# Sum columns ordered by kind, so that a product between two graph layers skips its zero blocks

## The chip, the cores and the metric

One NeuronCore of one Trainium2 chip runs the whole program. The metric is the time of one execution on the device in microseconds. The kernel before takes 9425.36 us (median of three runs, 9407.82 to 9427.2). Engines are named as in the profile: PE is TensorE (PEld its weight loads), DVE is VectorE, ACT is ScalarE, POOL is GpSimd, SP is SyncE.

## What is computed

Two message-passing layers over a graph of 12500 nodes with 160 features (64 scalars and 32 vectors of 3) and 212500 edges. Cut to what matters, the first layer is:

```python
h = max(layernorm(x), 0)                       # per node
f0, f1 = h_scalars @ Wl1_0, h_vectors @ Wl1_1  # per node
w = silu(edge_scalars @ Wfc1) @ Wfc2           # per edge, 192 numbers: w0, w1, w2, w3
mid0 = w0 * f0[src] * sh0                      # 64 scalars          -> n0
mid1 = w3 * sum_m(f1[src] * sh1) / sqrt(3)     # 32 scalars          -> n1
mid2 = w1 * f0[src] x sh1                      # 64 vectors of 3     -> n2
mid3 = w2 * f1[src] * sh0                      # 32 vectors of 3     -> n3
n0..n3 = sums over the edges of a node / max(count, 1)
scal, vec = [n0, n1], [n2, n3]
alpha = scal @ Wa                              # 1 number
conv = [scal @ Wl2_s, vec @ Wl2_v per m]       # 64 and 3 x 32 numbers
x = x + skip(h) + alpha * conv
```

So the scalar outputs (and alpha) come from the scalar sums alone, and component m of the vector outputs from component m of the vector sums alone. The second layer has the same form with other products.

## The kernel before

The program runs in stages. First the edges are sorted by node for the first layer (`sort_edges`): GpSimd scatters edge rows, with their filter weights already computed, to DRAM with indirect DMAs. Then `messages` of the first layer goes over 928 tiles of 256 edges: VectorE makes a one-hot matrix of the edges' nodes and products of weights and gathered features in the tile `prod`, ScalarE makes the outer products (L1689), and TensorE sums them by node (L1637), 449 columns at once: these are the sum columns. VectorE adds the results up in `acc`, and ScalarE's queue stores them as rows of `agg_tab`. Beside that GpSimd gathers features (L1554) and already scatters three quarters of the second layer's edge rows (L1571).

The stage between the layers, `middle`, handles 98 blocks of 128 nodes and, with them, the last 52 chunks (1024 edges each) of the second layer's sort. One step is one block; a chunk is spread over two steps, an even and an odd one. In each step a block's sums (449 columns, padded with zeros to 512) are transposed in four pieces of 128 columns (L1169), moved to SBUF by ScalarE (L1223), and multiplied with `w_out0` (L1178): four f32 products that accumulate 161 output columns, each against 128 rows of weights. Most of these weights are zeros, because each sum column feeds only some outputs. VectorE makes the scale alpha from output column 160 (L1377), adds the outputs to x (L1384, L1385), and takes the layer norm of the new x (L1348, L1359, L1371); TensorE turns the result (L1187, L1188) and makes the node features (L1195, L1196).

The order on each engine is fixed by the code: TensorE's step is transposes of block b, for an even step the rank counts (L416) and the hidden product of the next chunk (L1130), product of block b-1 (L1178), two weight products of the chunk's halves (L488), node turn of block b-3, node product of block b-4. VectorE's step begins with `prepare`: in an even step the bin products, their sum, the next bin one-hot and its count (L350, L360, L330, L341), about 5 us; in an odd step small operations. Then come count, statistics, alpha and `add_conv` of block b-1. There is one PSUM bank for the outputs, so a product waits for `x_done`, VectorE's last use of the one before; alpha waits for `mm_ready`, the product. ScalarE evicts the weight products (L1229), and GpSimd then scatters the chunk with 8 indirect DMAs (L1119).

Which sum column stands where is set by names: in the kernel before, columns 0 to 95 are mid3, 96 to 159 mid0, 160 the count (`ones_at`), 161 to 352 mid2 (`outer_at`), 353 to 448 mid1 (`inner_at`). The weight rows are placed accordingly by `weight_loads`; its helper `rows_into` splits a block of weights that crosses a multiple of 128 rows into two DMAs. SyncE issues these DMAs (L597) at the start, ahead of the sort's first edge data. The last product of the second layer, in `node_sums` (L2011), already runs on column ranges (`L1.spans`), ten passes a block.

Of the kernel before, what the change touches and what calls it, by code (L numbers as in the profile page):

```python
# [21 lines left out]
ALU = mybir.AluOpType  # L22
# [57 lines left out]
S0, V0 = 64, 96  # L80
D = S0 + V0
# [9 lines left out]
L0 = Layer()  # L91
# [4 lines left out]
L0.skip_cols = (64, 96)  # L96
L0.agg = 449
L0.pw = 452
L0.ones_at, L0.outer_at, L0.inner_at = 160, 161, 353
L0.out_cols = 161  # L100
L0.kchunks = [128] * 4
L0.hot_bufs, L0.prod_bufs, L0.res_bufs, L0.add_lag = 4, 4, 3, 4
L0.accs, L0.stores, L0.store_lag = 6, 2, 6

# [134 lines left out]
def weight_loads(t, g):  # L239

    placed = []

    def rows_into(l, row, src, col):

        n, done = src.shape[0], 0
        while done < n:
            r = row + done
            k = min(n - done, P - r % P)
            placed.append((g.w_out[l.n][r % P:r % P + k, r // P, col:col + src.shape[1]], src[done:done + k, :]))
            done += k  # L250

    rows_into(L0, 96, t["L0_gnn_Wl2_s"][0:64, :], 0)
    rows_into(L0, 96, t["L0_gnn_Wa"][0:64, :], 160)
    for m in range(3):
        rows_into(L0, 32 * m, t["L0_gnn_Wl2_v"][64:96, :], 64 + 32 * m)
        rows_into(L0, L0.outer_at + 64 * m, t["L0_gnn_Wl2_v"][0:64, :], 64 + 32 * m)
        rows_into(L0, L0.inner_at + 32 * m, t["L0_gnn_Wl2_s"][64:96, :], 0)
        rows_into(L0, L0.inner_at + 32 * m, t["L0_gnn_Wa"][64:96, :], 160)
    sums_row = lambda group, q: 320 * L1.bank_of[group] + 64 * q + 32 * L1.turn_of[group]
    for q in range(2):  # L260
        rows_into(L1, sums_row(0, q), t["L1_gnn_W_out_s"][32 * q:32 * q + 32, :], 0)
    for k in range(3):
        rows_into(L1, sums_row(0, 2 + k), t["L1_gnn_W_out_v"][64:96, :], 96 + 32 * k)
        for q, (what, j) in enumerate(L1.hots[k][0::2]):
            row = sums_row(k + 1, q)
            if what == "p":
                rows_into(L1, row, t["L1_gnn_W_out_v"][32 * j:32 * j + 32, :], 96 + 32 * k)
            elif what == "3":
                rows_into(L1, row, t["L1_gnn_W_out_s"][64:96, :], 0)
            else:  # L270
                i = 3 - j - k
                plus = (i, j, k) in ((0, 1, 2), (1, 2, 0), (2, 0, 1))
                rows_into(L1, row, t["L1_gnn_W_out_v"][96:128, :] if plus else g.neg_cross[:, :], 96 + 32 * i)
    for l, (feat, skip) in ((L0, ("L0_gnn_Wl1_1", "L0_gnn_Wsc1")), (L1, ("L1_gnn_W_nl1", "L1_gnn_W_skip1"))):
        for m in range(3):
            placed.append((g.wn_v[l.n][m:V0:3, 32 * m:32 * m + 32], t[feat]))
            placed.append((g.wn_v[l.n][m:V0:3, V0 + 32 * m:V0 + 32 * m + 32], t[skip]))
    fc = []
    for l, name1, name2 in ((L0, "L0_gnn_Wfc1", "L0_gnn_Wfc2"), (L1, "L1_gnn_W_fc1", "L1_gnn_W_fc2")):
        for h in range(2):  # L280
            fc.append((g.w1[l.n][h * l.fc_in:(h + 1) * l.fc_in, 64 * h:64 * h + 64], t[name1]))
            col = 0
            for a, b in l.w_cols:
                fc.append((g.w2[l.n][64 * h:64 * h + 64, col:col + b - a], t[name2][:, a:b]))
                col += b - a
    plain = [(g.wn_s[0][:, 0:S0], t["L0_gnn_Wl1_0"]), (g.wn_s[0][:, S0:], t["L0_gnn_Wsc0"]),
             (g.wn_s[1][:, L1.skip_cols[0]:], t["L1_gnn_W_nl0"]), (g.wn_s[1][:, 0:L1.skip_cols[0]], t["L1_gnn_W_skip0"])]
    return fc, plain, placed
# [702 lines left out]
def middle(nc, t, g):  # L991
# [3 lines left out]
    nk = len(L0.kchunks)  # L995
# [15 lines left out]
    with ExitStack() as ctx:  # L1011
# [7 lines left out]
        aggT = [sb(f"aggT{s}", [P, nk, P], F32) for s in range(2)]  # L1019
# [30 lines left out]
        agg_bank, res = g.ps2[1][:, 0, :], g.ps2[1][:, 1, :]  # L1050
# [76 lines left out]
        def _(pe):  # L1127
# [44 lines left out]
            def product(step, it, s):  # L1172
                b = it * DEEP + s
                pe.wait_ge(aT_ready, b + 1)
                if step is None or step >= 1:
                    pe.wait_ge(x_done, b)
                for k, n in enumerate(L0.kchunks):
                    mm = pe.matmul(res[:, 0:L0.out_cols], aggT[s % 2][0:n, k, :], g.w_out[0][0:n, k, :],  # L1178
                                   start=(k == 0), stop=(k == nk - 1))
                mm.then_inc(mm_ready, 1)  # L1180

            def node_turn(step, it, s):
# [106 lines left out]
        def _(dve):  # L1289
# [89 lines left out]
            def add_conv(step, it, s):  # L1379
                b, c, _ = held(step, it, s)  # L1380
                dve.wait_ge(chain, 4 * b + 4)
                xs = g.x_sb[:, bass.ds(b, 1), 0:S0].rearrange("p o d -> p (o d)")
                xv = g.x_sb[:, bass.ds(b, 1), S0:D].rearrange("p o (v m) -> p (o m) v", m=3)
                dve.scalar_tensor_tensor(xs, res[:, 0:S0], c[:, 3:4], xs, ALU.mult, ALU.add)  # L1384
                dve.scalar_tensor_tensor(xv, res[:, S0:D].rearrange("p (m v) -> p m v", m=3), c[:, 3:4], xv,  # L1385
                                         ALU.mult, ALU.add).then_inc(x_done, 1)

            def inverse_root(step, it, s):
# [21 lines left out]
def messages(nc, t, l, g):  # L1410
# [3 lines left out]
    with ExitStack() as ctx:  # L1414
# [3 lines left out]
        def sem(name):  # L1418
# [13 lines left out]
        hot_ready, hot_scaled, prod_ready, sum_ready, acc_ready, iota_made = (  # L1432
            sem(x) for x in ("hot_ready", "hot_scaled", "prod_ready", "sum_ready", "acc_ready", "iota_made"))
        if sends:
# [24 lines left out]
            res = [b[:, 0:l.agg].rearrange("p (o c) -> p o c", o=1)  # L1459
                   for b in (g.ps[0], g.ps[1], g.ps2[1][:, 0, :])]  # L1460
# [319 lines left out]
        def _(dve):  # L1780
# [112 lines left out]
            def other_products(step, it, s):  # L1893
                u = it * TURN + s
                out_p = prod[s % prods]
                _, _, scalars, vectors = forms(s)
                if sends:
                    half = part[s % 2]
                    vectors(0, 0, 0, 3, 1)
                    scalars(32, 96, 1).then_inc(prod_ready, 1)  # L1900
                    dve.wait_ge(part_ready, u * 2 + 2)
                    dve.tensor_tensor(  # L1902
                        out_p[:, :, l.inner_at:l.inner_at + V0].rearrange("p k (m c) -> p k m c", m=3),
                        half[:, :, S0:].rearrange("p k (m c) -> p k m c", m=3),
                        rows[s % HELD][:, :, l.sh_at:l.sh_at + 3].bitcast(F32).rearrange("p k (m o) -> p k m o", o=1)
                        .to_broadcast([P, ST_TILES, 3, 32]), ALU.mult).then_inc(inner_ready, 1)
                else:
                    p0 = l.pieces_at
                    vectors(192, p0, 0, 3, 3)
                    vectors(160, p0 + 160, 0, 2, 3)  # L1910
                    vectors(160, p0 + 32, 2, 3, 1).then_inc(prod_ready, 1)
# [262 lines left out]
```

## Time and profile before

| | |
|---|---|
| Time, median of three runs | 9425.36 us (9407.82 to 9427.2) |
| Span of the profiled execution | 9425.4 us |
| Time of the profiled execution | 9425.36 us |
| Mean granted TensorE clock | 0.831 |
| Sort of the first layer | to about 2200 us |
| First layer's messages | about 2230 to 6150 us |
| Between the layers | about 6180 to 6780 us |
| Second layer's messages | about 6830 to 9230 us |
| Second layer's node sums | to the end |

The profile is one execution. Busy times of engines overlap, so they don't add up to the span. A row of a group gives busy time and mean duration, then the idle time of its engine just before these instructions and what ended it ("<-issue" where no wait explains it). A matmul's duration includes the time to run through the array, so that several in a row start closer together than they last. The granted clock is the share of TensorE's full speed: 1.0 is 2.4 GHz and 0.5 is 1.2 GHz.

### The profile page before, as it was taken

To read this page: it belongs to the slowest core of one execution; us is meant where nothing else is said; L and a number is where in the kernel's file an instruction comes from. 1 tells how busy PE (TensorE), PEld (TensorE's weight loads), DVE (VectorE), ACT (ScalarE), POOL (GpSimd) and SP (SyncE) were. 2 spreads that over 40 slices of the span, in tenths; PEclk is the share of its full clock that TensorE was granted. 3 is DMA by queue.
4 is the path that set the end of the run, shared out by engine and by line. 5 is a ranking of instruction groups with operands and counts; after the bars stand their busy time and mean duration, and the time that the engine had idled before them with its cause. 6 is when DMAs were issued, how large, how long until landed. Compare 5 with 4: busy or idle time off the path is not lost. (4 is left out here: it accounts for less than half of the span.)

```text
span 9425.4 us, 173139 instructions
## 1 busy us (share of the span) xinstructions
PE 6599.8 (70%) x31166; PEld 4418.9 (47%) x31166; DVE 7175.1 (76%) x21240; ACT 4951.0 (53%) x16490; POOL 6782.0 (72%) x6877
## 2 busy tenths in 40 slices
PE   5566565654655565555555556678799999999999
PEld 3333333332222222222222222356588888888888
DVE  7666666665777676767777778977699999999995
ACT  3444444443444444444444445644477777777774
POOL 5777777777777777777777776456677777777770
PEclk7565555657888888888888888989899999999999
DMA  3222222225666666666666666545556666666667
GB/s 105 93 91 93 92 92 92 92 90 165 212 215 212 212 211 213 212 212 212 212 213 214 212 213 205 182 146 171 155 165 167 167 169 168 167 168 169 170 167 229
DMA packets 1189742, 1589.17 MB, mean 169 GB/s; under 512 B 452520, under 2 KB 967336, under 8 KB 1189544
## 3 DMA queue, kind: packets, MB, share of 16 engines
q1 hardware_dynamic: 789976, 836.56, 29.0%
q0 software_dynamic: 328704, 651.74, 24.2%
q10 hardware_dynamic: 70992, 100.14, 3.0%
q8 instruction: 20, 0.33, 0.0%
q14 instruction: 50, 0.41, 0.0%
HBM read 999.62 MB, written 1050.39 MB: 217 GB/s over the span
## 5 line engine op out<-in xcount | busy, mean ns | idle before, releaser
L1656 PE MATMUL pair<-prod_m,hot_m 128*128 128x160 f32 x14848 | 2245.1, 304 | 164.3 <-DVE prod_m L1862 128.1
L1543 POOL DMA_INDIRECT feat_m<-feat_tab,rows_m x1856 | 1830.9, 986 | 579.0 <-issue 441.9
L1656 PEld LDWEIGHTS pair<-prod_m,hot_m 128*128 128x128 f32 x14848 | 2043.6, 190 | 365.9 <-issue 361.3
L1677 ACT ACTIVATE hot_m<-hot_m,rows_m 128x128 f32<-128x128 f32 x5568 | 1728.5, 389 | 700.7 <-DVE hot_m L1845 694.8
L1554 POOL DMA_INDIRECT fetched_m<-feat_tab,index_m x1664 | 1673.2, 1006 | 518.5 <-issue 501.2
L663 POOL DMA_INDIRECT sorted_rows<-rows_e,place_e x1664 | 1611.6, 969 | 539.5 <-issue 503.9
L1689 ACT ACTIVATE prod_m<-part_m,rows_m 128x64 f32<-128x64 f32 x5568 | 1432.3, 337 | 1018.6 <-DVE part_m L1882 864.9
L1571 POOL DMA_INDIRECT sorted_rows<-later_m,place_m x1248 | 1243.9, 997 | 523.8 <-issue 376.4
L1637 PE MATMUL bank<-prod_m,hot_m 128*128 128x449 f32 x2476 | 1111.8, 572 | 575.6 <-DVE prod_m L1902 320.9
L1862 DVE TENSOR_TENSOR prod_m<-rows_m,feat_m 128x192 f32<-128x192 f32 (+2 forms) x4640 | 1282.7, 308 | 0.0
L488 PE MATMUL pair<-fc,hT_m 64*128 64x224 f32 x2496 | 405.5, 454 | 963.8 <-ACT later_m L1732 952.2
L1637 PEld LDWEIGHTS bank<-prod_m,hot_m 128*128 128x128 f32 x2476 | 435.7, 195 | 1304.0 <-issue 1075.4
L1923 DVE SCALAR_TENSOR_TENSOR acc_m<-acc_m,same_block,pair 128x640 f32<-128x640 f32 (+1 forms) x1237 | 1016.8, 822 | 2.3 <-PE pair L1656 2.2
L1732 ACT ACTIVATE later_m<-pair 128x448 f32<-128x448 f32 x624 | 301.8, 535 | 1077.6 <-DMA sorted_rows<-later_m,place_m 1074.7
L488 PEld LDWEIGHTS pair<-fc,hT_m 64*128 64x128 f32 x2496 | 262.5, 228 | 1185.4 <-ACT later_m L1732 1035.9
L1855 DVE TENSOR_TENSOR prod_m<-rows_m,feat_m 128x128 f32<-128x128 f32 x2784 | 709.1, 281 | 101.0 <-DMA feat_m<-feat_tab,rows_m 99.2
L1831 DVE CAST later_m<-meta_m 128x8 f32<-128x8 int32 x156 | 31.3, 200 | 946.8 <-DMA sorted_rows<-later_m,place_m 946.8
L1637 PE MATMUL pair<-prod_m,hot_m 128*128 128x449 f32 x1236 | 720.3, 717 | 39.2 <-DVE prod_m L1902 37.7
L488 PE MATMUL pair<-fc,hT_e 64*128 64x192 f32 x3328 | 602.2, 539 | 0.8 <-ACT rows_e L692 0.8
L416 PE MATMUL bank<-bin_count_e,upper_bf 128*128 128x100 bf16 x207 | 53.5, 259 | 780.5 <-DVE bin_prod_e L350 780.5
L488 PEld LDWEIGHTS pair<-fc,hT_e 64*128 64x128 f32 x3328 | 499.5, 324 | 198.2 <-issue 197.5
L1119 POOL DMA_INDIRECT sorted_rows<-later_c,place_c x416 | 415.3, 998 | 219.5 <-issue 123.0
(264 smaller groups left out, 10303.2 us busy)
## 6 DMA issues: line engine op xcount, KB each, us to landing
agg_tab<-acc_m ACTq DMA_DIRECT2D x928, 320.0 KB
rows_m<-sorted_rows SPq DMA_DIRECT2D x928, 229.0 KB
agg_tab<-acc_m ACTq DMA_DIRECT2D x928, 224.5 KB
rows_m<-sorted_rows SPq DMA_DIRECT2D x928, 197.0 KB
feat_m<-feat_sorted SPq DMA_DIRECT2D x928, 160.0 KB
feat_sorted<-fetched_m SPq DMA_DIRECT2D x208, 640.0 KB, 5.3
turned_m<-in_turned ACTq DMA_DIRECT2D x159, 256.0 KB
agg_s<-agg_tab SPq DMA_DIRECT2D x98, 320.0 KB
```

Source lines behind the costliest of these rows:

```text
L488: return pe.matmul(out, hT[h, k % HALF * P:(k % HALF + 1) * P], g.w2[l.n][h, :], start=True, stop=True)
L663: pool.indirect_dma_start(out=g.sorted_rows[0], out_offset=bass.IndirectOffsetOnAxis(ap=place[s][:, k:k + 1], axis=0), in_=rows[s][:, k, : ...
L1543: pool.indirect_dma_start(out=feat[s % RING][:, k, :], out_offset=None, in_=g.feat_tab[l.n], in_offset=bass.IndirectOffsetOnAxis(ap=rows[s ...
L1554: pool.indirect_dma_start(out=fetched[q][:, k, :], out_offset=None, in_=g.feat_tab[0], in_offset=bass.IndirectOffsetOnAxis(ap=index[q][:, ...
L1571: pool.indirect_dma_start(out=g.sorted_rows[1], out_offset=bass.IndirectOffsetOnAxis(ap=place[h][:, k:k + 1], axis=0), in_=later[h][:, k, ...
L1637: mm = pe.matmul(out[:, 0, :], hot[s % l.hot_bufs][:, k, 0, :], prod[s % prods][:, k, 0:l.agg], start=(k == 0), stop=(k == ST_TILES - 1))
L1656: mm = pe.matmul(dst, hot[s % l.hot_bufs][:, k, q, :], rhs, start=(k == 0 and q < 2), stop=(k == ST_TILES - 1), skip_group_check=True)
L1677: ins = act.activation(hot[s % l.hot_bufs][:, k, 1 + q, :], hot[s % l.hot_bufs][:, k, 0, :], ACT.Copy, scale=rows[s % HELD][:, k, l.sh_at ...
L1689: ins = act.activation(prod[s % prods][:, k, at:at + S0], part[s % 2][:, k, 0:S0], ACT.Copy, scale=rows[s % HELD][:, k, l.sh_at + m:l.sh_a ...
L1855: return dve.tensor_tensor(out_p[:, :, pcol:pcol + 64 * d].rearrange("p k (q c) -> p k q c", q=2)[:, :, :, 0:32], w[:, :, wcol:wcol + 64]. ...
L1862: return dve.tensor_tensor(out_p[:, :, pcol:pcol + 32 * d * n].rearrange("p k (m c) -> p k m c", m=n)[:, :, :, 0:32], w[:, :, wcol:wcol + ...
L1923: dve.scalar_tensor_tensor(half(acc[q]), half(prev), same, res[s % l.res_bufs], ALU.mult, ALU.add).then_inc(acc_ready, 1)
```

## The change

The sum columns are put in another order: mid2 (outer) in 0 to 191, mid3 in 192 to 287 (`vec_at`), mid1 (inner) in 288 to 383, mid0 in 384 to 447 (`scal_at`) and the count in 448. The outputs are reordered too: the 96 vector outputs come first, then the 64 scalar outputs, then alpha's column 160. Each piece of 128 sum columns now reaches only a range of outputs, and the product is limited to it: 64, 96, 97 and 65 columns, 322 in all, where it was four times 161. The first product starts the accumulation with only the first 64 output columns. VectorE's operations and the weight placement follow the new order.

```diff
-L0.ones_at, L0.outer_at, L0.inner_at = 160, 161, 353
+L0.ones_at, L0.outer_at, L0.vec_at, L0.inner_at, L0.scal_at = 448, 0, 192, 288, 384
 L0.out_cols = 161
 L0.kchunks = [128] * 4
+L0.spans = [(0, 64), (0, 96), (64, 161), (96, 161)]
...
-    rows_into(L0, 96, t["L0_gnn_Wl2_s"][0:64, :], 0)
-    rows_into(L0, 96, t["L0_gnn_Wa"][0:64, :], 160)
+    rows_into(L0, L0.scal_at, t["L0_gnn_Wl2_s"][0:64, :], V0)
+    rows_into(L0, L0.scal_at, t["L0_gnn_Wa"][0:64, :], D)
     for m in range(3):
-        rows_into(L0, 32 * m, t["L0_gnn_Wl2_v"][64:96, :], 64 + 32 * m)
-        rows_into(L0, L0.outer_at + 64 * m, t["L0_gnn_Wl2_v"][0:64, :], 64 + 32 * m)
-        rows_into(L0, L0.inner_at + 32 * m, t["L0_gnn_Wl2_s"][64:96, :], 0)
+        rows_into(L0, L0.vec_at + 32 * m, t["L0_gnn_Wl2_v"][64:96, :], 32 * m)
+        rows_into(L0, L0.outer_at + 64 * m, t["L0_gnn_Wl2_v"][0:64, :], 32 * m)
+        rows_into(L0, L0.inner_at + 32 * m, t["L0_gnn_Wl2_s"][64:96, :], V0)
         rows_into(L0, L0.inner_at + 32 * m, t["L0_gnn_Wa"][64:96, :], 160)
...
-                    mm = pe.matmul(res[:, 0:L0.out_cols], aggT[s % 2][0:n, k, :], g.w_out[0][0:n, k, :],
-                                   start=(k == 0), stop=(k == nk - 1))
+                    a, z = L0.spans[k]
+                    mm = pe.matmul(res[:, a:z], aggT[s % 2][0:n, k, :], g.w_out[0][0:n, k, a:z],
+                                   start=(k == 0), stop=(k == nk - 1), skip_group_check=True)
...
-                dve.scalar_tensor_tensor(xs, res[:, 0:S0], c[:, 3:4], xs, ALU.mult, ALU.add)
-                dve.scalar_tensor_tensor(xv, res[:, S0:D].rearrange("p (m v) -> p m v", m=3), c[:, 3:4], xv,
+                dve.scalar_tensor_tensor(xs, res[:, V0:D], c[:, 3:4], xs, ALU.mult, ALU.add)
+                dve.scalar_tensor_tensor(xv, res[:, 0:V0].rearrange("p (m v) -> p m v", m=3), c[:, 3:4], xv,
...
-                    vectors(0, 0, 0, 3, 1)
-                    scalars(32, 96, 1).then_inc(prod_ready, 1)
+                    vectors(0, l.vec_at, 0, 3, 1)
+                    scalars(32, l.scal_at, 1).then_inc(prod_ready, 1)
```

## Rows read from the trace of the kernel before

**Rows 1.** Page, part 1: busy time, share of the span, instructions per engine.

```profile
PE 6599.8 (70%) x31166; PEld 4418.9 (47%) x31166; DVE 7175.1 (76%) x21240; ACT 4951.0 (53%) x16490; POOL 6782.0 (72%) x6877
```

**Rows 2.** Busy time by stage: PE, PEld, DVE, ACT, POOL, then clock, DMA, GB/s.

```profile
2230.00:6150.00 3920.00, 2349.53 (x6812) 1036.15 (x6812) 2896.01 (x8441) 1822.69 (x6658) 2894.02 (x2889) 0.85 0.68 210
...
6180.00:6780.00 600.00, 498.11 (x2776) 361.08 (x2775) 459.15 (x1616) 282.01 (x745) 394.31 (x396) 0.91 0.55 166
```

**Rows 3.** The costliest groups of the whole span: GpSimd's scatters.

```profile
L663 POOL DMA_INDIRECT sorted_rows<-rows_e,place_e x1664 | 1611.6, 969 | 539.5 <-issue 503.9
...
L1119 POOL DMA_INDIRECT sorted_rows<-later_c,place_c x416 | 415.3, 998 | 219.5 <-issue 123.0
```

**Rows 4.** Who waited for whom, 6170 to 6800 us: total, times, longest.

```profile
POOL sorted_rows L1119 <- ACT later_c L1229: 91.4, 35, 15.0
...
DVE bin_prod_c L350 <- PE bank L416: 70.5, 51, 3.9
...
PE pair L1178 <- DVE x_sb L1385: 53.1, 36, 3.0
...
DVE cnt_c L1377 <- PE pair L1178: 32.8, 47, 2.5
```

**Rows 5.** Timeline of an odd step at full clock: start, duration, instruction, idle before.

```profile
6434.78 1.34 PE L1178 MATMUL pair<-w_out,aggT_c 128*128 128x161 f32 x8 [0.83 <-DVE x_sb L1385]
...
6436.05 1.03 PE L488 MATMUL pair<-fc,hT_c 64*128 64x224 f32 x8
...
6436.16 0.28 DVE L1377 TENSOR_SCALAR cnt_c<-pair,cnt_c 128x1 f32<-128x1 f32 x1 [0.24 <-PE pair L1178]
...
6439.19 0.99 DVE L350 TENSOR_TENSOR bin_prod_c<-bin_hot_c,bank 128x800 f32<-128x800 bf16 x1 [0.46 <-PE bank L416]
```

**Rows 6.** Timeline of an odd step at half clock.

```profile
6408.80 2.48 PE L1178 MATMUL pair<-w_out,aggT_c 128*128 128x161 f32 x8 [2.12 <-DVE x_sb L1385]
```

**Rows 7.** Busy time of three whole cycles, product to product, columns as before.

```profile
6408.80:6423.59 14.79, 13.48 (x56) 9.62 (x57) 9.63 (x37) 5.76 (x16) 9.61 (x10) 0.67 0.50 154
...
6423.59:6434.78 11.19, 9.13 (x56) 6.63 (x57) 8.76 (x34) 5.70 (x17) 6.49 (x6) 1.00 0.57 161
...
6434.78:6446.15 11.37, 9.11 (x57) 6.63 (x57) 9.70 (x37) 5.67 (x16) 8.56 (x9) 1.00 0.63 190
```

**Rows 8.** Groups of instructions: both products, with counts, durations, first and last starts.

```profile
L1178 PE MATMUL pair<-w_out,aggT_c 128*128 128x161 f32 x784 | 146.1, 335 | 53.1 <-DVE x_sb L1385 53.1
...
L1178 PE MATMUL pair<-w_out,aggT_c x784: 297/301/608, 6183.2 to 6766.8; 128*128 128x161 f32 x196
...
L2011 PE MATMUL bank<-w_out,aggT_s 128*128 128x160 f32 x392 | 88.6, 308 | 0.0
...
L2011 PE MATMUL bank<-w_out,aggT_s 128*128 128x96 f32 x588 | 78.9, 270 | 0.0
```

**Rows 9.** Timeline: an even step's product, and the second layer's last, one block each.

```profile
6402.68 1.26 PE L1178 MATMUL pair<-w_out,aggT_c 128*128 128x161 f32 x8
...
9300.26 1.38 PE L2011 MATMUL bank<-w_out,aggT_s 128*128 128x160 f32 x10
```

**Rows 10.** Timeline of the start: weight DMAs, first wait for data, first scatter.

```profile
33.93 0.80 SPq L597 DMA_DIRECT2D w_out<-in_L_gnn_Wl_s  x2
...
41.78 0.42 SPq L597 DMA_DIRECT2D w_out<-in_L_gnn_Wa  x1
...
63.81 0.17 DVE L800 COPY first_sh_e<-meta_e 128x8 f32<-128x8 f32 x1 [2.29 <-DMA meta_e<-in_meta]
...
84.07 1.14 POOL L663 DMA_INDIRECT sorted_rows<-rows_e,place_e  x1 [30.30 <-DVE rows_e L803]
```

**Rows 11.** Groups in the first layer's messages: writes to even and odd columns.

```profile
L1902 DVE TENSOR_TENSOR prod_m<-part_m,rows_m 128x192 f32<-128x192 f32 x928 | 325.1, 350 | 0.0
...
L1883 DVE TENSOR_TENSOR part_m<-rows_m,feat_m 128x192 f32<-128x192 f32 x928 | 324.7, 350 | 0.0
...
L1689 ACT ACTIVATE prod_m<-part_m,rows_m 128x64 f32<-128x64 f32 x5568 | 1432.3, 337 | 1018.6 <-DVE part_m L1882 864.9
```

## The prediction

> **What bounds the kernel now.** I read the totals of the page first [rows 1]. VectorE, TensorE and GpSimd are each busy for 70 to 76% of the span, which says only that different stages have different limits, so next came the busy time by stage [rows 2]. The change touches two stages with its steady work: the first layer's messages (2230 to 6150 us) and the stage between the layers (about 6180 to 6780 us).
>
> In the sort before them and in the first layer's messages GpSimd is the limit. One indirect DMA of the sort takes 969 ns and the idle time before the 1664 of them is nearly all "issue", 503.9 us or 0.30 us each [rows 3]: 1664 x 1.27 = 2116 us, the whole stage. In the messages GpSimd has 2889 operations for 2894 us [rows 2]; with the same 0.30 us behind each that is 3761 of 3920 us. TensorE and VectorE have a quarter or more of their time free there.
>
> Between the layers no engine is full: in 600 us TensorE is busy 498, VectorE 459, GpSimd 394, and the granted clock is 0.91 [rows 2]. So it is a loop of waits, and the view to read is who waited for whom [rows 4]. GpSimd waits 35 times for ScalarE's eviction, 91.4 us. VectorE waits 51 times, 70.5 us, for the count products (L416), and 47 times, 32.8 us, for the product between the layers (L1178); TensorE in turn waits 36 times, 53.1 us, for VectorE's update of x (L1385) before that product. A cycle covers two blocks and one chunk. The timeline of one odd step shows the circle [rows 5]: the product starts at 6434.78 and is followed at once on TensorE by the weight products (6436.05), the node turns, the transposes and the counts, and VectorE's bin product (6439.19) waits for those counts. From there VectorE has some 7 us of its own work until it has updated x for the odd block, and only then can the next even block's product start. The first product starts at 6183.2 and the last at 6766.8 [rows 8]: 583.6 / 97 x 2 = 12.03 us per cycle, 49 cycles.
>
> Thus the product of an odd step (even blocks) lies on the loop with its full length: it is ahead of the counts on TensorE's queue. The product of an even step (odd blocks) runs beside VectorE's long work and is free, except where the clock is low.
>
> **Part 1: the product.** It is 8 passes (4 chunks of sums, and each f32 product is two passes: 784 for 98 blocks [rows 8]). At full clock the 8 take 1.26 us [rows 9] where a single one is 301 ns [rows 8]; right behind a wait they take 1.34 [rows 5]. The pace is (1.26 - 0.30) / 7 = 0.137 us a pass of 161 columns. Now the passes get 64, 96, 97 and 65 columns. How short can a pass be that must also load 128 columns of weights? The second layer's last product has the answer: 10 passes, four of 160 and six of 96 columns, take 1.38 us [rows 9], one lasts 0.27 to 0.31. That leaves 1.08 us for 9 intervals; three of them belong to 160 columns at 0.137, so the other six are (1.08 - 0.41) / 6 = 0.11 us. Scaling by columns would have given 0.08. So there is a floor from the weight loads, and passes of 64 columns lie on it too.
>
> Saved per product: 7 x (0.137 - 0.11) = 0.19 us, and 0.03 to 0.08 us at the end of the last pass, which is shorter (160 against 96 columns: 308 against 270 ns is the nearest comparison [rows 8]). I take 0.25 us. The bounds: zero, if the passes keep their pace, and 7 x 0.067 + 0.08 = 0.55 us, if a pass costs only its columns (0.137 / 161 = 0.00085 us each, 80 on average, half of today's pace). The value near the weight floor is nearest to an actual row of the same kind of product. The Trainium skill says the same of this floor: in "TensorE: Matmul & The Clock Gate", section "LDWEIGHTS (loading the stationary operand)", a load lasts its columns divided by 1.2, about 107 ns for 128; this trace agrees with its 0.11. The same page's step on filling the array says that throughput is N cycles; by that alone the saving would be the upper bound, and the row of 96 columns speaks against it.
>
> At half clock everything doubles (2.48 us for the product [rows 6]). All L1178 passes together are 146.1 us busy [rows 8], 1.49 per product against 1.26, so on average 1.18 times the full-clock price: 0.25 x 1.18 = 0.295 us. On the loop for 49 odd steps: **14.5 us**. About ten even steps at low clock also hold VectorE up (the 47 waits of L1377 are more than the 36 of TensorE on x): at half clock they save 0.5 us, of which VectorE's next cover takes some; I take 0.3 each, **3 us**.
>
> Does the saving get through? What is late next in an odd step is VectorE itself, whose small operations come until 0.24 us before L1377, and which in a full-clock cycle waits 0.46 us for the counts [rows 5]. Both branches start at the product's end, so both move. GpSimd needs 8 x (0.998 + 0.34) = 10.7 us a cycle [rows 3], and the shortest cycles are 11.19 us [rows 7]: 0.5 us of room, twice what a full-clock cycle gives back. It would cap the 0.55. The last three chunks have no blocks and go by GpSimd alone; they only start sooner.
>
> **Part 2: the first layer's sums.** The columns move inside a tile of the same width. The number of instructions, their shapes, the 449 columns of the sum products and the agg table's row stay. The only possible price is where writes start: ScalarE's outer products went to columns 161, 225, 289 and VectorE's inner product to 353, and now all start at multiples of 32. VectorE's inner product into column 353 takes 350 ns, and the same shape written into an even place (L1883) also 350 [rows 11]: zero. Were it to gain or lose 10 ns an operation, GpSimd would hide it: 26% of VectorE's time is free in that stage [rows 2]. The change of add and count reads (L1384, L1385, ones at 448) is the same shapes on another column: zero.
>
> **Part 3: the weight loads at the start.** Blocks of weights crossed a multiple of 128 rows and were loaded in two pieces. Counting from the code: 19 DMAs for the first layer's w_out before, 14 after. SyncE issues them from 33.93 to 42.20 us, 0.435 us each [rows 10]; behind them on its queue stand the second layer's weights and then the sort's first edge data, for which VectorE waits 2.29 us at 63.81 [rows 10]. Five fewer save at most 2.2 us, and at least about 1.0, since whole pieces take a little longer to issue than halves; I take **1.5 us**. From there the path goes over VectorE to GpSimd's first scatter at 84.07, and then GpSimd is full to the end of the messages, so this shift is kept.
>
> **Part 4: the clock.** TensorE's granted clock between the layers switches between 1.0 and 0.5 (2.4 and 1.2 GHz). A cycle at 1.00 takes 11.19 or 11.37 us, one with clock 0.67 took 14.79 [rows 7]. Before the product at half clock the engine had stood idle 2.12 us, before the one at full clock 0.83 [rows 5, 6]. The mean cycle is 12.03 against 11.28, so low clock costs (12.03 - 11.28) x 49 = 37 us now. The change takes about 0.5 us of work out of TensorE's 9.1 us per cycle and leaves the cycle 0.3 us shorter: idle goes from 2.1 to about 2.4 us, a seventh more. If the time lost to low clock grows in that proportion, it costs **5 us**; bounds: 15 us back (the shorter cycle meets the clock better) and 20 lost.
>
> **Sum.** 14.5 + 3 + 1.5 - 5 = 14 us. The profiled execution has a span of 9425.4 us, the time of the run is 9425.36, the median of the three (9407.8 to 9427.2), so nothing lies around it: 9425.4 - 14 = 9411 us, 0.15% less.
>
> **Rivals.** (a) *The clock does better, or the passes go below the weight floor.* For it: cycles vary from 11.2 to 14.8 with no change in work, and a shorter cycle may meet fewer idle stretches. Half of the 37 us back in place of 5 lost: 9425 - 19 - 18 = 9388; passes by columns alone, capped by GpSimd's 0.5 us: 9425 - 49 x 0.55 - 4 = 9394. Against: idle before the products grows, and the row of 96 columns. Chance 0.25 for this and for results of the forecast's own kind that land beyond 0.2%. (b) *The product is covered, or the clock takes all of it.* TensorE then waits for x that much longer, and the time is that of the shorter start, 9424, or 9420. Against: 47 waits of L1377 for the product and 51 for the counts. Chance 0.15. (c) *Slower, by the clock.* The mechanism: TensorE's stay between its transposes and the next product gets longer and more of the odd steps' products, weights and turns run at 0.5, each such cycle costing up to 3.5 us (14.79 - 11.28) [rows 7]. It decides from (19 + 19) / 37 x 0.09 = 0.09 less granted clock on, that is at 0.82 or lower; with 0.80 the stage costs 45 us more and the time is 9451. The Trainium skill has this rule in "TensorE: Matmul & The Clock Gate", section "HAM oscillation — how this bites in real kernels": gaps between groups of matmuls bring the clock back down. The trace agrees that low clock stands behind a gap (2.12 us, above); whether 0.3 us more makes many more of them no row shows. Chance 0.1. That the change doesn't shorten the passes at all is in (b).
>
> **Chances.** Forecast as summed (11 to 19 us less) 0.5, (b) 0.15, (a) 0.25, (c) 0.1. What a measurement of this kernel can tell from no change is about 0.2%, 19 us; the forecast and (b) lie within it. So faster 0.27, same 0.62, slower 0.11. Range: (a) down to 9390 and the start of (c), 9436, with the runs of before alone spreading over 19 us.
>
> **What would show it.** L1178: 784 passes still, busy down from 146 to 115 to 120 us, 8 in 1.0 us at full clock; if 0.8, the weight floor is wrong. Waits of L1377 fewer or shorter. Shortest cycles of 10.9 to 11.1 us. Granted clock of 6180 to 6780 between 0.87 and 0.93; outside it part 4 is wrong. The first messages' stage 3920 us as before with L1902 and L1689 at 350 and 337 ns. First scatter at 82 to 83 us. A stage time of the messages that differs by more than 10 us would make the forecast wrong for a reason that I don't have.

## The result and the profile after

The changed kernel takes 9451.99 us (median of 10 runs, 9429.79 to 9468.36), the kernel before 9421.31 us (median of 10, with the three known earlier). The ratio is 1.0028, 95% interval 1.002 to 1.0037: about 27 us slower (the two medians are 31 us apart). The forecast was 14 us less, 9411. The profiled execution has a span of 9459.7 us and took 9461.86, near the upper end of its runs.

First its busy time by stage (engines in the order of [rows 2], then clock, DMA share and GB/s):

```profile
2230.00:6150.00 3920.00, 2330.96 (x6775) 1026.70 (x6776) 2879.69 (x8397) 1812.47 (x6624) 2905.53 (x2885) 0.85 0.68 210
...
6180.00:6780.00 600.00, 493.89 (x2658) 357.57 (x2658) 442.62 (x1553) 271.32 (x708) 376.09 (x380) 0.82 0.54 162
```

Against [rows 2] the messages show the same clock and the same load. Between the layers TensorE is busy nearly as long as before (494 against 498 us) although its product got shorter, and the granted clock fell from 0.91 to 0.82. Next the product itself, in the groups of the whole span and in the list of its passes (least, median and greatest duration in ns, first and last start):

```profile
L1180 PE MATMUL pair<-w_out,aggT_c 128*128 128x97 f32 (+3 forms) x784 | 118.5, 302 | 49.9 <-DVE x_sb L1387 49.9
...
L1180 PE MATMUL pair<-w_out,aggT_c x784: 219/275/475, 6202.5 to 6793.1; 128*128 128x64 f32 x98, 128*128 128x97 f32 x98
```

784 passes, 118.5 us busy instead of 146.1 [rows 8]. But from the first to the last it is 590.6 us instead of 583.6. Then two whole cycles at full clock and two at low clock:

```profile
6637.36:6648.44 11.08, 8.58 (x57) 6.33 (x57) 9.74 (x37) 5.64 (x16) 6.67 (x8) 1.00 0.57 174
6648.44:6659.36 10.92, 8.60 (x57) 6.32 (x57) 8.77 (x34) 5.70 (x17) 7.66 (x8) 1.00 0.61 176
6543.01:6556.10 13.09, 11.62 (x56) 8.16 (x57) 8.76 (x34) 5.91 (x17) 6.09 (x6) 0.74 0.47 138
6556.10:6570.42 14.32, 13.97 (x57) 9.95 (x57) 10.72 (x43) 5.40 (x15) 10.59 (x11) 0.56 0.59 175
6488.55:6624.60 136.05, 119.11 (x561) 84.94 (x561) 91.30 (x319) 58.90 (x152) 76.31 (x79) 0.72 0.48 146
```

At full clock the cycle is 11.08 and 10.92 where [rows 7] has 11.37 and 11.19: the gain of 0.27 to 0.29 us is there. TensorE's idle time in such a cycle, the cycle less its busy time, was 2.1 and 2.3 us and is 2.5 and 2.3. The last row is what takes the gain away: ten cycles in a row with a mean clock of 0.72 and 13.6 us each. In the first profile of the kernel before the ten slowest cycles in a row last 12.2 us each (in the second profiles, e2 and e1 below, 12.9 for the change and 12.6 for the kernel before):

```profile
6192.64:6315.05 122.41, 103.31 (x556) 74.85 (x557) 90.84 (x326) 56.03 (x148) 80.74 (x81) 0.87 0.55 165
```

The timeline of an odd step at full clock:

```profile
6648.44 1.08 PE L1180 MATMUL pair<-w_out,aggT_c 128*128 128x64 f32 x8 [1.34 <-DVE x_sb L1387]
...
6649.44 1.03 PE L489 MATMUL pair<-fc,hT_c 64*128 64x224 f32 x8
...
6649.70 0.28 DVE L1379 TENSOR_SCALAR cnt_c<-pair,cnt_c 128x1 f32<-128x1 f32 x1
...
6652.47 0.99 DVE L351 TENSOR_TENSOR bin_prod_c<-bin_hot_c,bank 128x800 f32<-128x800 bf16 x1 [1.43 <-PE bank L417]
```

The product takes 1.08 instead of 1.34 us, the next work follows after 1.00 instead of 1.27 us [rows 5], and VectorE has no idle time ahead of L1379 any more; its wait for the counts (L351) is 1.43 us here and was 0.46. The first bracket is 1.34 us where that of [rows 5] is 0.83, but such waits vary from step to step: over the stage TensorE waited for x ahead of this product for 53.1 us before [rows 8] and 49.9 us now. What grew is its idle time in a whole full-clock cycle, above.

One more comparison. This execution is 34 us longer than the profiled one of before, but the stage between the layers accounts for 7, and 19 lie ahead of it. The last scatter of the first layer's messages starts at 6182.2, against 6163.4 before. So either the change costs something ahead of the product, or stages scatter between executions. That had to be told apart first.

### The profile page after: what moved, and what is told of

Its sections match the earlier page's. It is cut to its first block and busy times, and to the rows that moved or that the text cites. A ratio compares the mean times of both kernels' runs of the same rounds, so it can differ in the third digit from the quotient of the medians.

```text
span 9459.7 us, 173134 instructions
## 1 busy us (share of the span) xinstructions
PE 6607.8 (70%) x31166; PEld 4425.1 (47%) x31166; DVE 7179.7 (76%) x21240; ACT 4953.5 (52%) x16490; POOL 6805.2 (72%) x6877
```

## The experiments

Times are compared with runs of the kernel before on the same chip. "Stage" is the time from the first to the last pass of the product between the layers. The granted clock is that of 6200 to 6720 us, and "at half clock" is 2 x (1 - clock) x stage, since the clock is either 1.0 or 0.5: in windows of half a microsecond it reads one of the two, but for the windows in which it changes. Added up from such windows, the time at half clock is 109, 109, 99, 192, 188, 255, 140, 134, 7 and 0 us in the kernels of the table from the first to e6, and 120, 109 and 27 us in e9 to e11, so that the rounded clock does little harm. The stage's columns are of one profiled execution each, and several of these are among the slowest of their kernel's runs. The last column is of all timed runs: the time at half clock in the whole execution, 2 x (1 - mean clock) x span, averaged, less the same for the kernel before on the same chip, with its standard error.

| kernel | ratio (95% interval) | stage, us | clock | at half clock, us | timed runs, more at half clock, us |
|---|---|---|---|---|---|
| before, first profile | 1 | 583.6 | 0.91 | 105 | - |
| before again (e1) | 1.0003 (0.9994 to 1.0012) | 585.0 | 0.90 | 117 | +3 (9) |
| new order, full width (e3) | 1.0 (0.9991 to 1.0009) | 579.9 | 0.91 | 104 | +8 (11) |
| change, first profile | 1.0028 (1.002 to 1.0037) | 590.6 | 0.83 | 201 | - |
| change again (e2) | 1.003 (1.0018 to 1.0043) | 585.8 | 0.84 | 187 | +124 (14) |
| old order, narrow (e4) | 1.0028 (1.0019 to 1.0038) | 617.3 | 0.80 | 247 | +151 (14) |
| narrow in odd steps (e7) | 0.9991 (0.9982 to 0.9999) | 576.0 | 0.88 | 138 | +50 (10) |
| narrow in even steps (e8) | 1.0001 (0.9992 to 1.001) | 592.5 | 0.88 | 142 | +16 (14) |
| change, filled (e5) | 0.9952 (0.9939 to 0.9965) | 538.9 | 1.00 | 0 | -106 (8) |
| before, filled (e6) | 0.9962 (0.9949 to 0.9975) | 549.8 | 1.00 | 0 | -118 (11) |
| change, even steps filled, 2 (e9) | 0.9984 (0.9975 to 0.9993) | 572.9 | 0.90 | 115 | +7 (10) |
| change, odd steps filled, 3 (e10) | 1.0003 (0.9994 to 1.0012) | 582.0 | 0.90 | 116 | +32 (9) |
| change, even steps filled, 4 (e11) | 0.9958 (0.9945 to 0.9972) | 540.1 | 0.97 | 32 | -63 (8) |

**Which half of the change costs?** First the kernel before once more, with a profile of its own.

> The kernel before, unchanged, with a profile of its own: it shows how far two profiles of one kernel differ stage by stage, and gives the times to which the others of this group are compared. Theory P (the product between the layers and the clock cause the loss): the sort ends and the messages end within 5 us of where they did in the first profile. Theory N (the differences of 5 and 14 us in the stages ahead of the product come from the chip or the execution, not from the change): these stages differ from the first profile by as much as they do with the change, and GpSimd's common scatter of 961 ns is 961 to 963 here as well. Ratio to before 1.000 within its interval.

9416.94 against 9414.98 us. Here is the last scatter of the messages in this profile:

```profile
L1571 POOL DMA_INDIRECT sorted_rows<-later_m,place_m x1248: 954/961/1825, 2277.7 to 6171.6; - x179
```

It starts 8 us later than in the first profile of the same kernel (theory P had allowed 5), so this end scatters between executions. The changed kernel again:

> The changed kernel, unchanged, on the same chip as the kernel before. Theory P: 9440 to 9455 us, ratio 1.002 to 1.0035, and of this 8 us or more between the layers with a granted clock of 0.82 there (0.91 before). Theory N: most of the loss in total time is gone on this chip, ratio 0.999 to 1.001. Theory L (the layout of the first layer's sums costs in the messages): the messages take 10 us or more longer than in the kernel before on this chip.

9438.91 us, ratio 1.003. The total repeats; the messages do not:

```profile
L1573 POOL DMA_INDIRECT sorted_rows<-later_m,place_m x1248: 954/961/1753, 2277.7 to 6167.0; - x179
```

Theory N said that the loss in the total would go, and it stayed; theory L said that the messages get longer, and here they end 5 us earlier than in e1. What was right of N is only that the 19 us ahead of the product in the first profile were not the change's. Theory P's 8 us or more between the layers aren't in these two profiles either: the stage is 585.8 us here and 585.0 in e1. But e1's profiled execution is the slowest of its 11 runs and e2's the fastest of its 6 (9433.85 and 9430.63 us): one profile isn't the median. The timed runs have 124 us more at half clock than those of the kernel before. Then one half of the change at a time.

```diff
-                    a, z = L0.spans[k]
+                    a, z = 0, L0.out_cols
```

> The new order of the sum columns, but all four products take 161 columns as before. Theory P: the product has its old length, so the stage between the layers takes as long as in the kernel before and the granted clock there is 0.88 or more; ratio 0.999 to 1.001. Theory L: as slow as the changed kernel, ratio about 1.003, with the loss in the messages.

9415.81 us, ratio 1.0.

```profile
L1573 POOL DMA_INDIRECT sorted_rows<-later_m,place_m x1248: 954/961/1759, 2278.1 to 6181.4; - x179
```

This execution reaches the end of the messages as late as the changed kernel's first one did, without any loss in the timed runs. The order of the columns costs and gains nothing that can be measured; theory L falls. The other half, on the kernel before:

```diff
-                    mm = pe.matmul(res[:, 0:L0.out_cols], aggT[s % 2][0:n, k, :], g.w_out[0][0:n, k, :],
-                                   start=(k == 0), stop=(k == nk - 1))
+                    a, z = ((0, 64), (0, 96), (64, 161), (96, 161))[k]
+                    mm = pe.matmul(res[:, a:z], aggT[s % 2][0:n, k, :], g.w_out[0][0:n, k, a:z],
+                                   start=(k == 0), stop=(k == nk - 1), skip_group_check=True)
```

> The old order of the sums, but the four products take 64, 96, 97 and 65 columns. It leaves out parts of the product, so the outputs are not those of the reference; the time and the waits are those of a narrow product. Theory P: ratio 1.002 to 1.0035, the granted clock between the layers 0.82 to 0.86, as with the change. Theory L: ratio 0.998 to 1.000.

9444.71 us, 1.0028: the whole loss comes with the narrow product. (This kernel leaves out parts of the product, so that only its time counts.) The messages start their last scatter at 6165.3 us in this trace, 2 us from the first profile of before, and the stage is 617.3 us; this execution is the slowest of its 10 runs:

```profile
6200.00:6720.00 520.00, 441.42 (x2300) 317.72 (x2300) 380.57 (x1335) 236.03 (x615) 322.18 (x330) 0.80 0.54 162
```

Who waited for whom in this stage (total, times, longest):

```profile
POOL sorted_rows L1119 <- ACT later_c L1230: 117.6, 37, 6.6
...
DVE bin_prod_c L350 <- PE bank L416: 99.8, 46, 3.9
```

These are the waits of [rows 4], with 91.4 and 70.5 us there (the first of them holds a wait of 15.0 us that lies ahead of this view). VectorE waits more for the counts, which come out of TensorE's queue behind the product, although the product is shorter. The reading is that the rest of that queue runs at the lower clock; the filled kernels below test it.

**Is it the clock or a wait that goes with it?** A theory of the clock must survive this: give TensorE more work in its idle time, and the kernel must become faster. The filling products multiply the identity with itself (f32, two passes each of 128 columns) into the bank of the hidden product.

```diff
+            def fill(n):
+                for _ in range(n):
+                    pe.matmul(hid[:, 0:P], g.ident[:, :], g.ident[:, :], start=True, stop=True, skip_group_check=True)
+
+            def odd_fill(step, it, s):
+                w = chunk(step, it, s, 1)
+                if w is not None and (step is None or step < MID_STEPS - 2):
+                    pe.wait_ge(hT_ready, w[0] + 2)
+                    fill(3)
...
                 behind(0, trans)(step, it, s)
+                odd_fill(step, it, s)
                 counts(step, it, s)
...
                     pe.wait_ge(hT_ready, c + 1)
+                    fill(4)
```

> The changed kernel with idle TensorE time between the layers filled: 3 products of 128 columns by 128 behind the transposes of an odd step and 4 behind the counts of an even step, into a bank that nobody reads then. Their results are not used; the outputs are the reference's. Theory C (the loss comes from longer half-clock stretches, which follow TensorE's idle time): the granted clock between the layers goes to 0.97 or more, nearly every cycle takes 10.9 to 11.0 us, the stage loses 45 us and the ratio to the kernel before is 0.995. Theory W (the loss comes from waits that the narrow product opens elsewhere, and the low clock only goes with it): more work on TensorE makes it no faster, ratio 1.002 or more.

> The kernel before with the same filling products. Theory C: clock 0.97 or more, cycles of 11.2 us, 35 us less in the stage, ratio 0.996; the difference to the filled changed kernel is what the narrow product is worth when the clock is the same in both, 49 x 0.26 = 13 us. Theory W: ratio 1.000 or more.

9384.42 and 9390.08 us; the kernel before took 9423.17. Two cycles of the filled changed kernel, and its passes:

```profile
6453.02:6463.92 10.90, 10.14 (x70) 7.95 (x71) 8.74 (x34) 5.62 (x17) 7.54 (x8) 1.00 0.59 177
6463.92:6475.04 11.12, 10.09 (x71) 7.95 (x71) 9.78 (x37) 5.58 (x16) 8.57 (x9) 1.00 0.66 194
...
L1181 PE MATMUL pair<-w_out,aggT_c x784: 219/275/474, 6185.4 to 6724.3; 128*128 128x64 f32 x98, 128*128 128x97 f32 x98
```

and those of the filled kernel before:

```profile
L1179 PE MATMUL pair<-w_out,aggT_c x784: 297/300/376, 6178.5 to 6728.3; 128*128 128x161 f32 x196
```

In the first fence TensorE has 10.1 us of work in a cycle of 10.9 to 11.1 where it had 8.6, and the cycle is no longer. The clock stays at 1.00 from 6200 to 6720 us. Theory W falls: more work on the engine makes the stage 52 us shorter (590.6 to 538.9). The stages of the two filled kernels, 538.9 and 549.8 us, give what the narrow product is worth when the clock is out of it: 10.9 us, 0.22 a cycle (forecast 0.25, or 12 us for 49 cycles). Their timed runs differ by 0.001 in the ratio and 5.7 us in the medians, the same order, but their intervals overlap, so the total alone doesn't show it.

**Less work, or a shorter cycle?** Both could lengthen the time at half clock. They part if the product is narrow in one kind of step alone, because only the odd step's product is on the loop.

```diff
-                    a, z = L0.spans[k]
+                    a, z = L0.spans[k] if s % 2 == 0 else (0, L0.out_cols)
```

Here `s` is that of the block; even blocks have their product in odd steps. The second kernel has `s % 2 == 1`.

> The changed kernel with the narrow product in odd steps alone (even blocks, the ones on the loop); in even steps each product takes 161 columns. Full-clock cycles 10.92 us in every theory. Theory A (less work on TensorE in a cycle lengthens the half-clock stretches): half of the lost work is back, so 140 to 170 us at half clock between the layers, about 15 us less lost than with the change, ratio 1.000 to 1.002. Theory B (the length of the cycle decides, by how it falls against the clock): as much time at half clock as with the change, 190 us or more, ratio 1.003.

> The narrow product in even steps alone (odd blocks, beside VectorE's long work); in odd steps 161 columns. Full-clock cycles stay at 11.18 us in every theory. Theory A: 140 to 170 us at half clock and nothing gained on the loop, ratio 1.001 to 1.003. Theory B: the cycle is as long as in the kernel before, so 115 us at half clock and ratio 1.000.

9414.11 and 9425.31 us against 9423.17. The windows of both, in this order:

```profile
6200.00:6720.00 520.00, 437.91 (x2432) 319.51 (x2432) 400.31 (x1424) 246.74 (x654) 346.43 (x350) 0.88 0.57 170
```

```profile
6200.00:6720.00 520.00, 424.43 (x2369) 309.83 (x2368) 388.57 (x1378) 240.62 (x634) 332.22 (x337) 0.88 0.55 164
```

Both profiles have a clock of 0.88 and about 140 us at half clock, between the 105 to 117 of a wide product and the 187 to 247 of a narrow one. The shortest ordinary cycles are 10.83 to 10.93 us in e7, as with the change, and 11.11 to 11.20 in e8, as in the kernel before (11.10 to 11.19): only the odd step's product is on the loop.

Theory B wanted 190 us or more and a ratio of 1.003 in e7; it has 138 us and 0.9991, so theory B fails there. Theory A is close, and a shade too dark: it had 140 us and 1.000 as its best. With the product narrow in odd steps the gain on the loop and the loss by the clock nearly cancel, with a slight gain.

In e8 the two sources disagree. The profiled execution has 142 us at half clock and a stage of 592.5 us, as theory A has it, but it is one of the three slowest of the 12 runs (9445.11 us). All 12 together have a ratio of 1.0001 and only 16 us more at half clock than the kernel before, with a standard error of 14, and that is what theory B had forecast (1.000). So e8 doesn't show that less work in even steps alone costs anything. The two halves together cost 124 us at half clock, more than the halves apart (50 and 16): the clock's answer to less work is not linear. That the length of the cycle plays no part at all isn't shown by this pair; e9 and e11 below, which keep the short cycle and put work back, show that work is what brings the clock back.

**How much work, and where?** TensorE has two idle stretches in a cycle. The prediction looked at one, ahead of the odd step's product, where TensorE waits for x. The other is in the even step, ahead of the hidden product (L1130), where it waits for the DMA of `turned_c`. In the kernel before it is nearly as large as the one for x, which has 53.1 us [rows 4] (total, times, longest):

```profile
PE bank L1130 <- DMA turned_c<-in_turned: 47.9, 36, 2.9
```

The last three kernels fill one of them alone: 2 or 4 products behind the counts of even steps, right ahead of the hidden product, or 3 behind the transposes of odd steps, in the idle stretch ahead of the product. The edit of e9 against the filled changed kernel; e10 has `fill(3)` and `fill(0)`, e11 `fill(0)` and `fill(4)`:

```diff
-                    fill(3)
+                    fill(0)
...
-                    fill(4)
+                    fill(2)
```

> The changed kernel with 2 filling products (4 passes, about 0.43 us) behind the counts of an even step and none in odd steps: about as much work per cycle as the change took away (0.5 us), but off the loop. Theory A (time at half clock follows the work on TensorE in a cycle): 100 to 125 us at half clock between the layers as in the kernel before, with full-clock cycles of 10.92: 12 us gained, ratio 0.998 to 0.9995. Theory G (only the idle stretch right ahead of the odd step's product counts, and this one is as long as with the change or longer): 190 us or more at half clock, ratio 1.003.

> The changed kernel with the 3 filling products in odd steps alone, behind the transposes, in the idle stretch ahead of the product. Theory A: more work than before the change (0.65 us added against 0.5 taken away), so less than 114 us at half clock, ratio 0.996 to 0.998. Theory G: this stretch is the cause, so nearly full clock, ratio 0.9955 as with both fills.

> The changed kernel with the 4 filling products in even steps alone (0.86 us). Theory A: fewer than 80 us at half clock, ratio 0.996 to 0.998. Theory G: 190 us or more at half clock, ratio 1.003.

9402.11, 9418.84 and 9382.9 us against 9416.62. Their windows, in this order:

```profile
6200.00:6720.00 520.00, 444.29 (x2640) 329.56 (x2639) 405.06 (x1427) 250.12 (x660) 347.54 (x354) 0.90 0.58 173
```

```profile
6200.00:6720.00 520.00, 434.13 (x2637) 330.02 (x2636) 396.55 (x1398) 241.62 (x640) 343.48 (x345) 0.90 0.56 168
```

```profile
6200.00:6720.00 520.00, 454.31 (x2970) 344.48 (x2968) 429.50 (x1506) 262.10 (x696) 372.41 (x373) 0.97 0.61 181
```

Two filling products, about as much work as the change took away, bring the clock back to 0.90 and leave the gain of the shorter cycle: 0.9984. That is theory A, and against G, which had 1.003. Four bring it to 0.97 and the ratio to 0.9958. The miss is e10: 3 products in odd steps are more work than 2 in even steps and gave the same clock of 0.90, but a ratio of 1.0003 where 0.996 to 0.998 was expected; its stage is 9 us longer than that of e9. The timed runs say the same: 32 us more at half clock than in the kernel before, against 7 in e9. So the amount of work alone does not decide; the place does too. The idle time of TensorE from 6200 to 6720 us shows part of why, first e9, then e10:

```profile
PE pair L1181 <- DVE x_sb L1399: 40.3, 41, 2.1
PE bank L1131 <- DMA turned_c<-in_turned: 35.0, 28, 3.5
```

```profile
PE bank L1131 <- DMA turned_c<-in_turned: 47.7, 25, 3.6
PE pair L1181 <- DVE x_sb L1399: 37.9, 24, 2.6
```

The stretch ahead of the hidden product stays open in e10, with 1.9 us a wait. Of the 23 falls of the clock from 1.0 to 0.5 in e10's stage, 19 came in or behind this stretch, with no other wait between; of the 18 in e9's, 15 came behind the wait for x. Behind such a wait in e10 the hidden product and the even step's product run at half clock (the hidden product takes 2.05 us at 6405.11 where it takes 1.09 at 6415.60), and VectorE waits for that product 31 times, 44.1 us in all, where it is 12 times and 10.7 us in e9. In the kernel before the falls are shared: of 24, 13 came with the wait for x and 11 with the other. A microsecond at half clock is dearer there, too: against the full-clock stage of 538.9 us e10 lost (582.0 - 538.9) / 116 = 0.37 us for each, e9 (572.9 - 538.9) / 115 = 0.30. Whether the place of the half-clock stretches makes the whole difference, no run isolates.

The filled kernels with 4 products in even steps are the fastest that were run: with or without the odd steps' 3, 34 to 39 us below the kernel before (the filled kernel before: 33).

## Why the prediction was wrong, point by point

**What bounds the stage.** Right. It is a loop over TensorE and VectorE, GpSimd sets the stages before it, and the product of an odd step is on the loop: narrowing it alone (e7) shortens the full-clock cycle, narrowing the other (e8) does not. One term was taken too high: GpSimd's 0.34 us between scatters is 0.30 without its waits for the eviction, so that the room was more than 0.5 us; the filled cycles of 10.90 us show that it capped nothing.

**The product (part 1).** Right, in its pieces. A product takes 1.08 us where it took 1.34, and a median pass 275 ns where it took 301. Of the forecast range of 0 to 0.55 us, 0.26 was measured and 0.25 taken. Its busy time is 118.5 us (115 to 120 forecast), the shortest ordinary cycles are 10.83 to 10.93 us (10.9 to 11.1) where those of before are 11.10 to 11.19. At equal clock the stage shows 10.9 us of gain against 14.5 summed; the factor of 1.18 for low clock has no place there, and 49 x 0.25 = 12 is the number to compare. The extra 3 us for even steps at low clock can't be seen apart.

**The first layer's sums (part 2).** Right: ratio 1.0 with the new order at full width (e3).

**The start (part 3).** Right in kind, smaller in size. Here are the first wait and the first scatter after:

```profile
63.18 0.17 DVE L801 COPY first_sh_e<-meta_e 128x8 f32<-128x8 f32 x1 [1.64 <-DMA meta_e<-in_meta]
...
83.45 1.14 POOL L664 DMA_INDIRECT sorted_rows<-rows_e,place_e  x1 [29.66 <-DVE rows_e L804]
```

0.6 us earlier than in [rows 10], where 1.5 was taken from a range of 1.0 to 2.2, so it is below the range. The 14 DMAs are issued from 34.32 to 41.78 us, 0.53 us each where the 19 took 0.44: the whole pieces take longer to issue, and the first starts 0.39 us later.

**The clock (part 4).** This is the step that failed, and by its size. The mechanism was named: TensorE's idle time in a full-clock cycle grows, from about 2.2 to 2.4 us as forecast, and with it the time at half clock. The prediction's own sign for this part, a clock of 0.87 to 0.93 from 6180 to 6780 us, was missed with 0.82. It had let the time at half clock grow "in that proportion", a seventh for a seventh more idle time, and took 5 us for it. In the profiles it was 105 to 117 us and is 187 to 247, so 60% to 135% more, and by 124 us in the timed runs (e2). The clock falls about as often as before; what grew is how long it stays down. In windows of half a microsecond the stage has 24, 26 and 22 stretches of low clock with the wide product (before, e1, e3), 4.2 to 4.6 us each on average, and 26, 29 and 32 with the narrow one (change, e2, e4), 6.5 to 8.0 us each.

What it costs can be read by taking away the full-clock stage, 549.8 us for a wide and 538.9 for a narrow product: before, (583.6 - 549.8) / 105 = 0.32 us for each us at half clock; change (590.6 - 538.9) / 201 = 0.26; e4 (617.3 - 538.9) / 247 = 0.32; e8 (592.5 - 549.8) / 142 = 0.30. The changes in the timed runs give much the same: e2 (24 us lost and 11 gained) / 124 = 0.28, the filled kernel before 33 / 118 = 0.28, e11 (34 - 11) / 63 = 0.36. The price per microsecond at half clock changes little; the amount does. So the clock cost 35 us (e2) to 38 us (27 lost and 11 gained), where 5 were forecast.

So rival (c) happened, "slower, by the clock". It put its decision at a granted clock of 0.82 or lower, and the stage's clock in the first profile is 0.82 (0.84 in e2). That its 9451 us meet the measured 9452 is in part luck: it reckoned with a clock of 0.80, 45 us lost by it and 19 gained, and both were less, the gain 11. It had a chance of 0.1, and the range ended at 9436, because the proportion was taken for a law: the rows of before held the clock's price but not how steeply the time at half clock depends on the work. The upper bound of part 4, 20 us lost, was drawn from nothing in the rows, and it was the bound that had to hold.

The rule of the Trainium skill that gaps between groups of matmuls bring the clock down ("TensorE: Matmul & The Clock Gate", section "HAM oscillation — how this bites in real kernels") was cited and given too little weight. The runs agree with it: the filled kernels, with the gaps taken up, have a clock of 1.00 from 6200 to 6720 us and mean cycles of 11.1 us (change) and 11.3 us (before).

What stays open: how much of the difference between e9 and e10 is the place of the half-clock stretches, whether less work in even steps alone costs anything (e8's profile and its timed runs differ), and why the clock's answer is so steep. The first profile's late messages need no cause in the change: over the 13 profiles the last scatter of the messages starts between 6157.4 and 6182.2 us, with no relation to the order of the columns or the width of the product.

## What to carry to other kernels

Where TensorE waits in a loop and its granted clock is already between the two levels, a shorter product has two effects: it shortens the loop by what it saves, and it lengthens the time at half clock, which acts on all of the engine's work in the loop. Cost the second from the stage's own clock, and don't assume it in proportion: here 0.5 us less work in a cycle of 11 gave back 11 us and cost 35 to 38. If the work can't be kept, list all idle stretches of TensorE in the loop, put useless products into those off the loop, and measure which stretch.

## What the runs showed of the hardware

- A pass of an f32 product with 128 columns of weights stops getting shorter somewhere between 161 and 97 columns of data: with half the columns, eight passes took 1.08 instead of 1.34 us, as a floor of 0.11 us a pass gives it, and not 0.8.
- The time at half clock between the layers: 104 to 117 us with 9.1 us of TensorE work in a full-clock cycle, 187 to 247 with 8.6, and next to none (0 to 7) with 10.1. With one of the two products narrow the profiles have 138 to 142.
- A microsecond of this stage at half clock cost 0.26 to 0.37 us of time, in the profiles and in the timed runs.
- With a shorter product the clock fell about as often (26 to 32 times against 22 to 26) and stayed down longer (6.5 to 8.0 us against 4.2 to 4.6 on average).
- An execution's time up to the end of the first layer's messages scatters by 25 us (last scatter at 6157.4 to 6182.2 us in 13 profiles).
- Where the clock fell depended on which idle stretch was left open: with the stretch ahead of the hidden product filled (e9) 15 of 18 falls came behind the wait for x, with the stretch of that wait filled (e10) 19 of 23 came in or behind the one ahead of the hidden product.
